# Sender rows of two tiles gathered by SyncE through registers instead of by GpSimd

## The reference: one graph layer, a residual and a layer norm

```
edge_feat = concat([h[dst], h[src], rel_pos, distance])      # receiver, sender, 4 numbers
x = silu(edge_feat @ W1 + b1); x = silu(x @ W2 + b2)
scores = (x @ W3 + b3)[:, 0]
alpha = softmax of scores over the edges of one receiver
msg = h[src] @ Wv * (alpha * node_weight[src])
out = h + segment_sum(msg, receiver)
result = layernorm(h + out)
```

## Time and profile before

| | before |
|---|---|
| time, median of 3 runs | 998.13 us (997.67 to 998.24) |
| span of the profiled execution | 996.1 us |
| first sender gather | 3.04 us |
| first receiver gather | 250.75 us |
| first record gather | 300.81 us |

### The profile page before, as it was taken

One profiled execution on the slowest core, in us unless ns is written; L12 is line 12 of the kernel. 1 busy time (PEld: TensorE's weight loads), 2 busy tenths in 40 slices (PEclk: granted clock), 3 DMA queues, 4 the chain that ended last, 5 costly groups with the idle time before them and its releaser, 6 DMA issues.

```text
span 996.1 us, 10941 instructions
## 1 busy us (share of the span) xinstructions
PE 575.9 (58%) x2587; PEld 394.8 (40%) x2587; DVE 573.2 (58%) x2275; ACT 522.6 (52%) x1168; POOL 752.3 (76%) x790
## 2 busy tenths in 40 slices
PE   0989999988704457677667666777996600000000
PEld 0656766665502223455445444545675500000000
DVE  6987887773452737597698987953678841000000
ACT  0356655554523756777698979974786630000000
POOL 6777777777777777777777777777777777777777
PEclk9999999999998776788788988878999855555555
DMA  7799999989965877788778878763452231111111
GB/s 208 227 302 315 321 320 333 336 233 311 330 226 161 288 256 245 273 292 268 273 272 283 292 234 317 246 185 91 129 124 79 71 78 53 53 51 52 53 53 45
DMA packets 85079, 206.12 MB, mean 207 GB/s; under 512 B 19797, under 2 KB 56566, under 8 KB 72472
## 3 DMA queue, kind: packets, MB, share of 16 engines
q1 hardware_dynamic: 56728, 140.95, 41.7%
q0 software_dynamic: 28288, 64.48, 22.8%
HBM read 113.16 MB, written 92.31 MB: 206 GB/s over the span
## 4 chain that ended last, share of the span: by engine, by line
POOL 38%; issue 23%; PE 20%; ACT 13%; DVE 5%; DMA 0%; POOLq 0%; ACTq 0%; DVEq 0%
POOL hk L422 23%; POOL out_rows L426 15%; ACT xin L478 6%; PE bank L622 5%; PE bank L638 4%; PE bank L645 3%; PE bank L624 2%; ACT hk L530 2%; PE bank L616 2%; PE bank L609 2%; ACT hkT L501 1%; ACT x L511 1%; ACT zs L521 1%; PE bank L597 1%; DVE dst L899 1%
## 5 line engine op out<-in xcount | busy, mean ns | idle before, releaser
L478 ACT ACTIVATE xin<-xin,drs 128x128 f32<-128x128 f32 x637 | 258.1, 484 | 51.6 <-DVE drs L884 51.5
L422 POOL DMA_INDIRECT hk<-in_xw,snd_t x196 | 188.0, 959 | 62.0 <-issue 59.4
L426 POOL DMA_INDIRECT out_rows<-hk,sidx_t x196 | 188.8, 963 | 59.7 <-issue 59.4
L422 POOL DMA_INDIRECT region<-rec_d,id_t x196 | 186.8, 953 | 59.7 <-issue 59.1
L422 POOL DMA_INDIRECT hk<-in_x,kg_t x196 | 186.6, 952 | 59.7 <-issue 59.7
L899 DVE BATCH_NORM_STATS2 dst<-xin 128x6 f32<-128x256 f32 x392 | 137.0, 414 | 61.6 <-DMA xin<-in_x 61.0
L577 PE MATMUL bank<-w1b,region 128*128 128x128 f32 x392 | 149.1, 484 | 13.8 <-ACT region L488 7.8
L622 PE MATMUL bank<-hkT,w1a 128*128 128x512 f32 x98 | 73.2, 839 | 138.8 <-issue 98.3
L577 PEld LDWEIGHTS bank<-w1b,region 128*128 128x128 f32 x392 | 99.8, 315 | 33.9 <-ACT region L488 10.1
L622 PEld LDWEIGHTS bank<-hkT,w1a 128*128 128x128 f32 x98 | 20.1, 240 | 175.5 <-issue 163.2
L511 ACT ACTIVATE x<-bank,bcol 128x512 f32<-128x512 f32 x49 | 33.5, 683 | 95.0 <-PE bank L624 95.0
(11 more groups left out here) (176 smaller groups left out, 853.0 us busy)
## 6 DMA issues: line engine op xcount, KB each, us to landing
xin<-in_x SPq DMA_DIRECT2D x49, 1024.0 KB, 8.2
out_rows<-xin SPq DMA_DIRECT2D x49, 1024.0 KB, 5.2
rec_d<-hk SPq DMA_DIRECT2D x49, 514.0 KB, 7.7
krow<-seg_d SPq DMA_DIRECT2D x49, 128.0 KB, 3.5
hk<-in_xw,snd_t POOLq DMA_INDIRECT x196, 5.8
hk<-in_x,kg_t POOLq DMA_INDIRECT x196, 3.9
region<-rec_d,id_t POOLq DMA_INDIRECT x196, 3.6
out_rows<-hk,sidx_t POOLq DMA_INDIRECT x196, 2.2
```

The costliest lines, as they stand in the source:

```text
L422: pool.indirect_dma_start(out=to, out_offset=None, in_=frm, in_offset=bass.IndirectOffsetOnAxis(ap=index, axis=0)).then_inc(done, 16)
L426: pool.indirect_dma_start(out=out, out_offset=bass.IndirectOffsetOnAxis(ap=index, axis=0), in_=frm, in_offset=None).then_inc(done, 16)
L478: ins = nc.scalar.activation(xin[:, j % X_RING, n, :], xin[:, j % X_RING, n, :], ACT.Identity, bias=drs[:, j % 2, 1, n:n + 1], scale=drs[: ...
```

## The change

Tiles 193 and 194 (`OWN_TILES`), two of the four of the last group, leave GpSimd's list. SyncE fetches their 256 rows one by one. It loads 32 row numbers at a time into registers (`values_load_multi_w_load_instructions` on a new input `snd_own` that holds the same numbers), and issues for each a DMA of one row of `xw` to one partition, seven at the end of each turn from turn 4 on. Group 48 gets a thirteenth slot of its own (`slot`), so that its rows may come early, and GpSimd does not wait for a ring slot ahead of it. TensorE waits for both kinds of rows before the transposes of group 48.

```
+OWN_TILES = (T - 3, T - 2)
+OWN_READ, OWN_ROWS, OWN_FROM = 32, 7, 4
...
-        rec = hflat[:, G * GE - HS_RING * TPG * RW:].rearrange("p (r q w) -> p r q w", r=HS_RING, q=TPG)
+        rec = hflat[:, G * GE - (HS_RING + 1) * TPG * RW:].rearrange("p (r q w) -> p r q w", r=HS_RING + 1, q=TPG)
...
+        def slot(g):
+            return g % HS_RING if g < G - 1 else HS_RING
...
+            def sender_rows():
+                for o in range(0, len(OWN_TILES) * P, OWN_READ):
+                    _, rows = nc.values_load_multi_w_load_instructions(
+                        snd_own[0:1, o:o + OWN_READ], [mybir.EngineType.SP], min_val=0, max_val=N - 1,
+                        skip_runtime_bounds_check_because="senders are rows of x, those of the padding too")
+                    for n, r in enumerate(rows, o):
+                        q, p = OWN_TILES[n // P] % TPG, n % P
+                        sp.dma_start(rec[p:p + 1, slot(G - 1), q, H:RW], xw[bass.ds(r, 1), :]).then_inc(S["hs_rows"], 16)
+                        yield
...
                 dense(i)
+                for _ in range(OWN_ROWS if i >= OWN_FROM else 0):
+                    next(senders, None)
...
                 if kind == "hs":
-                    wait_ring(pool, rec_out, g - HS_RING, 16)
+                    if g < G - 1:
+                        wait_ring(pool, rec_out, g - HS_RING, 16)
                     for q in range(TPG):
                         t = g * TPG + q
-                        gather(rec[:, g % HS_RING, q, H:RW], xw, snd_t[:, t:t + 1], hs_in[g % HS_RING])
+                        if t not in OWN_TILES:
+                            gather(rec[:, slot(g), q, H:RW], xw, snd_t[:, t:t + 1], hs_in[g % HS_RING])
...
-                    wait_ring(pe, hs_in, i, 16 * TPG)
+                    if i == G - 1:
+                        pe.wait_ge(hs_in[i % HS_RING], 16 * (TPG * (i // HS_RING + 1) - len(OWN_TILES)))
+                        pe.wait_ge(S["hs_rows"], 16 * P * len(OWN_TILES))
+                    else:
+                        wait_ring(pe, hs_in, i, 16 * TPG)
...
+        "snd_own": snd[OWN_TILES[0] * P:(OWN_TILES[-1] + 1) * P].reshape(1, -1),
```

More of the change, by code:

```diff
@@ L116, in group_tiles, with gnn_kernel @@
     return min(BT, T - b * BT)
-def gnn_kernel(nc, x, xw, snd_nat, rcv_nat, id_nat, signs, iota, ef_flat, w1, b1, w2, b2, w3, b3, wv, eye, out):
+def gnn_kernel(nc, x, xw, snd_nat, snd_own, rcv_nat, id_nat, signs, iota, ef_flat, w1, b1, w2, b2, w3, b3, wv, eye, out):
     rec_d = nc.dram_tensor("rec_d", (EP, RW), F32).ap()
@@ L245, in gnn_kernel @@
             "parts_ready", "parts_out", "fix_ready", "fixT_done", "fexp_ready", "fexp_done", "fixY_ready", "fixY_done",
-            "fix_stats", "chain_f", "fix_res", "fix_out")}
+            "fix_stats", "chain_f", "fix_res", "fix_out", "hs_rows")}
         hs_in = [sem(f"hs_in{r}") for r in range(HS_RING)]
@@ L342, in write_rec @@
                 wait(sp, "rec_ready", j + 1)
-                sp.dma_start(rec_d[j * GE:(j + 1) * GE, :].rearrange("(q p) w -> p q w", p=P), rec[:, j % HS_RING]
+                sp.dma_start(rec_d[j * GE:(j + 1) * GE, :].rearrange("(q p) w -> p q w", p=P), rec[:, slot(j)]
                              ).then_inc(rec_out[j % HS_RING], 16)
@@ L360, in load_far @@
                 sp.dma_start(cont[0:n, b % FAR_RING, :], bass.AP(tensor=cont_d.tensor, offset=o, ap=[[P, n], [1, P]])).then_inc(to, 16)
+            def sender_rows():
[7 more added lines that the diff above has]
+                        yield
+            senders = sender_rows()
             for i in range(B0):
@@ L492, in _ @@
                     wait(act, "A_ready", j + 1)
-                    nc.scalar.activation(rec[:, j % HS_RING, :, 0:H], bank[2 + j % 4][:].rearrange("p (q h) -> p q h", q=TPG), ACT.Copy
+                    nc.scalar.activation(rec[:, slot(j), :, 0:H], bank[2 + j % 4][:].rearrange("p (q h) -> p q h", q=TPG), ACT.Copy
                                          ).then_inc(S["rec_ready"], 1)
@@ L580, in _ @@
                 if i < G:
-                    wait_ring(pe, hs_in, i, 16 * TPG)
+                    if i == G - 1:
[3 more added lines that the diff above has]
+                        wait_ring(pe, hs_in, i, 16 * TPG)
                     wait(pe, "hsT_ready", i - 1)
                     for q in range(TPG):
-                        ins = pe.transpose(bank[i % 2][:, q * P:(q + 1) * P], rec[:, i % HS_RING, q, H:2 * H], ident[:])
+                        ins = pe.transpose(bank[i % 2][:, q * P:(q + 1) * P], rec[:, slot(i), q, H:2 * H], ident[:])
                     ins.then_inc(S["T_ready"], 1)
```

## The result

The changed kernel takes 1024.32 us (median of 4 runs, 1024.05 to 1026.97), beside 997.90 us for the kernel before (4 runs, 997.66 to 998.24) on the same chip. The ratio is 1.0270, interval 1.0255 to 1.0284: 26.4 us slower. The profiled execution has a span of 1025.2 us against 996.1, so 29.1 us are to be found in it. It was the longest of the four, 2.6 us above the median.

A forecast was written before the change was run, and what follows sets the result against it. GpSimd, never idle, was taken to bound the kernel. Waiting 13 us for late record writes, less 2.5 gained, gives 10.5 on 998.1: 1008.6, plus 1 to 2 for DMA engines, 1010; own range 1000 to 1038, stated range 995 to 1045.

The forecast's parts named there:

- What bounds the kernel; gain of a gather: GpSimd never idles; each DMA taken off it brings the end 1.25 us nearer, two gathers 2.50 us.
- Row cost: On SyncE, a row takes 0.27 us issue, 0.05 address arithmetic and 0.19 number loading: 0.51 us, 3.6 us a turn.
- the step I trusted least: Loading row numbers on SyncE: three round trips a batch of 32, 6 us, or 0.19 us a row.
- SyncE's own work: SyncE's existing DMAs and pauses use 1.7 us of GpSimd's 5.0 us turn, leaving 3.3 us free.
- Waits that rows cannot fill: SyncE's waits within turns 4 to 40 that rows cannot fill: 0.25 us a turn, another 9 us.
- Nothing won back behind turn 41: The chain behind SyncE, some 29 us late at turn 41, gets not much shorter to the last record, TensorE being full.
- The cushion: Between the last record write's landing and record gather 0 at 300.81 us lie 16 to 21 us.
- One wait near 298 us: GpSimd shows one long wait for a record write near 298 us, 11 to 16 us, 13 in the middle.
- the dear case: Rival, chance 0.10: a row costs 0.83 us, SyncE 7.5 us a turn, end at 1070; sign: GpSimd waits among sender groups.
- The DMA engines: Extra load of 256 single-row packets on the sixteen full DMA engines adds 1 to 2 us.
- All hidden: Rival, chance 0.32: SyncE's idle time takes all rows, at 0.4 us or less each; end at 995.6 us.

The follow-up runs named there:

- two at the end: Kernel before, with two tiles of the last group scattered row by row by SyncE at the end, numbers from memory: 997.43 us beside 1000.28, ratio 0.9973.
- three at the end: Kernel before, with two tiles of the last group scattered row by row by SyncE and a third by ACT: 996.60 us, ratio 0.9959.
- four 4.2 of 5.0: Kernel before, with all four tiles of the last group scattered row by row, two by SyncE, two by ACT: 993.67 us beside 997.86, ratio 0.9959.
- six 5.7 of 7.5: Changed kernel with numbers from SBUF, six rows a turn, and four last-group tiles scattered by SyncE and ACT: 993.44 us beside 999.15, ratio 0.9936.
- loads alone: Changed kernel with all eight register-load batches, one row DMA each to a scratch, tiles filled by plain DMAs: 997.3 us beside 999.07, ratio 0.9983.
- fixed rows: Changed kernel with the 256 rows read from fixed addresses, no register loads or address arithmetic: 996.57 us beside 999.07, ratio 0.9976.
- one tile: Changed kernel with one tile instead of two on SyncE, four rows a turn instead of seven: 997.94 us beside 999.07, ratio 0.9992.
- SBUF, six: Changed kernel with row numbers read into registers from SBUF and six rows a turn instead of seven: 995.67 us beside 997.86, ratio 0.9976.
- SBUF, seven: Changed kernel, still seven rows a turn, with row numbers brought to SBUF once and read from there: 1004.93 us beside 1000.28, ratio 1.0053.
- memory, six: Changed kernel with six rows a turn instead of seven, numbers still from memory: 1012.87 us beside 1000.28, ratio 1.0131.
- SBUF, eight a load: Changed kernel with numbers from SBUF, seven rows a turn, loaded 8 at a time instead of 32: 1014.59 us beside 997.86, ratio 1.0159.
- 21 at a time: Changed kernel with 21 rows every third turn, behind the dense load, instead of seven every turn: 1045.53 us beside 999.07, ratio 1.046.

## Why the prediction missed its size

The direction and the mechanism were right, and the time lies in the range given; the 10.5 us of loss, 12 with the term for the DMA engines, became 26.4. Step by step:

- **What bounds the kernel; gain of a gather.** Right. 1.25 us each: two with free rows gave 2.50 us, two at the end 2.85, one 1.13, three at the end 3.68. Larger numbers gave less than their count: four 4.2 of 5.0, six 5.7 of 7.5.
- **Row cost, 0.27 + 0.05 + 0.19 = 0.51 us. This is the term that failed: it measured 0.66.** Loads: 0.175, a batch 5.6 us where I had taken 6, the step I trusted least. Address: two register instructions, not one pause, 0.15 from the pitch of 0.41 against 0.27. Issue: 0.34 in the mean instead of 0.27, as I had priced every row at the unblocked duration, though the earlier trace rows showed DMAs of this queue blocked. Over 256 rows the 0.15 us are 39 us of SyncE's time; the waits, put at 9 us where 2.5 were left, hid 7 of them by luck.
- **SyncE's own work, 1.7 a turn.** Right, 1.6.
- **Waits that rows cannot fill, 0.25 a turn.** Too high: 2.5 us in all, 0.07 a turn. 1.6 + 4.6 = 6.2 instead of 5.3 + 0.25; over 37 turns that is the difference between 29 us late and the 52.1 measured at the write of turn 41 (265.13 instead of 213.04).
- **Nothing won back behind turn 41.** Nearly right: 52.1 us late there, 47.3 at the last record. TensorE was indeed busy in that stretch, 47.5 of 55 us from 265 to 320; the slack of the window from 100 to 150 is over by then.
- **The cushion, 16 to 21 us.** Right. Before, the last record write landed 11.7 us after its issue, at 283.7, and 300.81 less that is 17.1 us. Of these the two gathers less take 2.5, so 14.6 are left. The write issued at 319.26 was waited for until 330.97, again 11.7 us. And 47.3 - 14.6 = 32.7 is what GpSimd lost up to record gather 0, where 11 to 16 were predicted, of which the 2.5 comes off.
- **One wait near 298 us, and a wait among sender groups as a sign of the dear case.** Wrong. The chain is 40 us late at record 24 already, so a ring of twelve slots is used up on the way: sixteen waits, 26.8 of 37.7 us. It does not add to the loss, as it is the same lateness paid in instalments, and the row's price was 0.66, not the 0.83 of that case. At 5.6 us a turn (six rows) the picture is the predicted one.
- **The DMA engines, 1 to 2 us.** Not there, no run shows this term: the kernel with 256 free-running rows got the whole 2.50 us. The term counted one packet for a row; the trace has two, one of the row's 516 bytes and one of 4, and still no cost is seen.
- **All hidden.** Fell for this kernel, right as a bound: 995.6 was the time at 0.33 us a row, and at 0.34 it came out 2.50 us under the kernel before.

The whole of it in one table: how late the last record write is issued, less 14.6 us of cushion, less 2.5 us gained, where positive (else the gain; 1.25 for one tile), beside the span less 996.1. The cushion is from the trace of the kernel before alone. The first column is SyncE's time for a turn, over the turns in which rows run, without its waits, read from each trace.

| kernel | us a turn | last write late | by that rule | measured |
|---|---|---|---|---|
| loads alone | 3.4 | 2.0 | -2.5 | -2.3 |
| fixed rows | 3.8 | 6.5 | -2.5 | -2.3 |
| one tile | 4.3 | 5.4 | -1.2 | -0.2 |
| SBUF, six | 4.8 | 11.8 | -2.5 | -2.2 |
| SBUF, seven | 5.4 | 21.0 | +3.9 | +3.4 |
| memory, six | 5.4 | 29.9 | +12.8 | +12.1 |
| SBUF, eight a load | 5.8 | 36.1 | +19.0 | +17.1 |
| changed kernel | 6.1 | 47.3 | +30.2 | +29.1 |
| 21 at a time | 6.6 | 66.9 | +49.8 | +50.0 |

The last two columns agree within 2 us: the lateness of one instruction on SyncE sets the time. Each row is one profiled execution. Those of SBUF seven and memory six were the fastest of four, their medians 3.5 and 2.7 us longer, and the kernel before itself took 1000.28 us beside them, so finer differences than 2 us say nothing.

Where rows run for 37 turns and SyncE is over 5 us a turn, its sum also gives the lateness. Its time without waits, less the 176.3 us that the kernel before took for these turns, is 50 us for the changed kernel, 24 for SBUF seven, 37 for eight a load and 67 for 21 at a time, beside 47.3, 21.0, 36.1 and 66.9 measured. With six rows from memory the same sum over 43 turns gives 23 us of the 29.9. What makes the rest, and the 2 to 12 us of lateness below 5 us a turn that the cushion swallows, stays open.

The Trainium skill, Runtime: NRT & Kernel Launch, "Instruction fetch mechanics", gives about 200 ns for each register loaded; measured were 175 ns from memory with the load of the address, and from SBUF 70 by the median batch and 88 by the mean. The rule was near for the one and two to three times too high for the other, and its estimate of 51 us led to the same forecast as my choice.

## What to carry to other kernels

Before work is put on a queue that seems idle, set its time for one turn, waits left out, against the turn of the engine that bounds the kernel, and price each item at the mean of that queue under load: 0.15 us too little on one row was 256 times too little, and the threshold was crossed with it. Below the threshold it cost nothing, a microsecond a turn above it cost the change thirty. Putting the items behind one another in long stops made it worse, since the queue's other DMAs then went out in a bunch and were blocked. So the cure was fewer items a turn and cheaper numbers, or a stretch in which the queue has nothing that anybody waits for. A ring of slots hides lateness only until it is used up, and then its owner pays in small waits long before the point where the last one is due.

## What the runs showed of the hardware

- A row DMA whose address comes from a register takes 0.41 us from one to the next on SyncE: 0.037 and 0.029 for two register instructions, 0.23 for the DMA and pauses between; beside other transfers 0.487 in the mean, and up to 1.00 where the issue is blocked.
- In the changed kernel, loading 32 registers from memory took 3.5 to 4.6 us and an address load of 1.0 to 2.2 ahead of it; from SBUF 2.25 us by the median, 0.81 for 8, without one. So by the medians one load from SBUF costs about 0.33 us and 0.06 a register; by the means, 2.82 and 1.11, about 0.5 and 0.07.
- Each row DMA moved as one packet of 516 bytes and one of 4 (256 more of each than before).
- With 21 rows at a time, and three turns' writes and loads issued in a bunch behind them, an edge load held SyncE 0.93 us in the mean, beside 0.51 in the changed kernel.
- ACT issues such rows as fast as SyncE: 0.48 and 0.52 us with their numbers.
